# One batch's token turns and the attention scores: the second token block moved behind the scores of step 6, and one maximum moved ahead of the keys' low part

## The chip, the core and the metric

The kernel runs on one core of one Trainium2 chip. The metric is the device time of one execution in microseconds (us); the figure quoted for a kernel is the median of its runs. An execution has five engines that work side by side, each through its own queue in order: TensorE (PE, with its weight loads shown apart as PEld), VectorE (DVE), ScalarE (ACT), GpSimd (POOL) and SyncE (SP), which here only issues DMAs. They wait for one another through semaphores.

## What is computed

Eight batches of 512 tokens of width 512 pass through a cross attention with 16 heads of 32, and then through a layer that mixes eight linear experts by a per-output router. Cut to what matters:

```
x = x + attention(layernorm(x), ctx, Wq, Wkv, Wout)
    qp = q @ Wq.T; k, v = split(ctx @ Wkv.T); per head: softmax(causal(q k^T / sqrt(32))) v; then @ Wout.T
x = x + mix(layernorm(x), router_w, router_b, expert_w, expert_b)
    logits = (h @ router_w.T + router_b).reshape(T, 512, 8); probs = softmax(logits)
    the two largest of eight per output, divided by their sum and added up over the outputs, weigh the eight experts' outputs
```

The causal mask lets query i see keys 0 to i, so only the first 512 context rows are used.

## The kernel before, in words

The attention stage takes about the first 640 us and is where the change lies; the router and expert stage follows, and the change doesn't touch it.

In the attention stage each batch b has four groups c = 0 to 3 of four heads (n = 4b + c counts groups). Each group has eight steps v = 0 to 7. The order on every engine is written by hand: each engine's `body` walks the same grid of (b, c, v) and issues its own share. Batches 1 to 5 are one loop body that the engines repeat (`Fori`), batch 0, 6 and 7 are written out.

All products with fp32 accuracy are made of three: each operand is split in a high part (a rounding, made by ScalarE) and a low part (the rest, made by VectorE). TensorE's three matmuls stand in L268 to L270.

What matters around the change, in c = 0 (`more` is true for batches 0 to 6):

- **First-pass scores** (`scores`, L673, mask matmul L679) run three steps ahead of the softmax. At step v they belong to the step that `target(c, v)` names, so "the scores of step 6" are those that are issued in v = 6. They fill one double bank, `s_ps`. VectorE takes each row's maximum from it (`maxima`, L1395 for masked steps), and the next scores wait for that (`negmax`), as there is just the one double bank.
- **Second-pass scores** (`shifted_scores`, L706) hold the maxima as extra rows; ScalarE takes their exponential (L1100).
- **Keys** of the group three ahead are made in v = 5 in bank 0 of `j_ps`. ScalarE copies their high part (L1017), VectorE makes the low part (`lo_of`, L1383).
- **Turned tokens**: in v = 6 and v = 7 of c = 0 the next batch's four blocks of 128 normalised tokens are transposed on TensorE (`turn_tokens`, `norm_turn`, L626, four matmuls a block). Block i goes to bank 1 - i % 2 of `j_ps`. ScalarE copies the high part (L1008), VectorE makes the low part (`turned_tokens`, L1371), and only then is the bank free. `TURNED` says which blocks in which step: 0 and 1 in v = 6, 2 and 3 in v = 7.
- **Banks**: `take(bank, task, k)` waits for what the bank held last. So block 0 (bank 1) waits for the queries' low part, block 1 (bank 0) for the keys' low part (`k_lo`), block 2 (bank 1) for the low part of block 0, and block 3 (bank 0) for the low part of block 1 (`xT_lo`).
- Behind block 3 in TensorE's queue stand the products with the values (`values_of`, L722), the sums (L734) and the scores of step 7.
- `lo_shift` (L1410) splits the turned maxima; SP's DMAs (L385) copy them into the rows of the second pass.

Of the kernel before, what the change touches and what calls it, by code (L numbers as in the profile page):

```python
# [28 lines left out]
QB = S // P  # L29
# [7 lines left out]
AHEAD = 3  # L37
# [8 lines left out]
def build(nc, x, ctxT, wqT, wkvT, woT, routerT, router_b, expertT, expert_b, out):  # L46
    ctx = ExitStack()
    with ctx:
# [228 lines left out]
        def masked(c, v):  # L277

            return v in (3, 4) or c == 0 and v > 4
# [11 lines left out]
        NORMALISED = ((2, 7), (3, 1), (3, 3), (3, 7))  # L291
        LAST_GROUP = {3: 0, 5: 1, 7: 2}
        TURNED = {6: (0, 1), 7: (2, 3)}
        OUT_BUF = (0, 1, 2, 0)
        INVERTED = 2
        REFINED = 3
# [16 lines left out]
        def key_rest(c):  # L313

            return {0: (0, 5), 1: (1, 7), 2: (2, 7), 3: (3, 7)}[c]
# [298 lines left out]
        def _(pe):  # L614
# [193 lines left out]
            def body(b, first, more, further):  # L808
                last = not more
                held = [("K", b * KC + AHEAD - 1), ("Q", b * KC + AHEAD - 1)]  # L810

                def take(bank, task, k):
                    freed(*held[bank])
                    held[bank] = (task, k)

                for c in range(KC):
                    n = b * KC + c
                    ahead = more or c == 0

                    def project(v):  # L820
                        i, chunk = out_block(c, v, last)
                        if i == 0:

                            pe.wait_ge(s["o_hi"], (b - 1) * KC + chunk + 1)
                            pe.wait_ge(s["o_lo"], (b - 1) * KC + chunk + 1)
                        if chunk == 0:
                            take(0, "WO", (b - 1) * QB + i)
                        project_out(b - 1, i, chunk, 0)

                    def turn_tokens(i):  # L830
                        take(1 - i % 2, "LNT", (b + 1) * QB + i)
                        norm_turn((b + 1) * QB + i, i, 1 - i % 2)

                    for v in range(UNITS):
                        out = not first and out_block(c, v, last) is not None
                        final = last and c == KC - 1
                        shifted_scores(n, c, v, final)
                        g, vv = target(c, v - 1)
                        if not masked((c if v else c - 1) % KC, (v - 1) % UNITS) and (more or c + g < KC):
                            scores(n + g, (c + g) % KC, vv, (1,))  # L840
                        if c == 0 and v in VALUE:
                            take(0, "V", b * QB + VALUE[v])
                            values(VALUE[v])
                        if v in QUERY and ahead:
                            if QUERY[v] == 0:
                                take(1, "Q", n + AHEAD)
                            queries(n + AHEAD, (c + AHEAD) % KC, QUERY[v])
                        if v == SUMMED and not (first and c == 0):
                            finish_group(n - 1, (c - 1) % KC, b if c else b - 1)
                        if final and v in LAST_GROUP:  # L850
                            last_group(LAST_GROUP[v])
                        if v == key_step(c) and ahead:
                            take(key_bank(c), "K", n + AHEAD)
                            keys((c + AHEAD) % KC, b if c == 0 else b + 1, key_bank(c))
                        if c == 0 and more:
                            for i in TURNED.get(v, ()):
                                turn_tokens(i)
                        if v == LAST and not final:
                            values_of(n, c, b, 0)
                            first_sums(n, more or c < KC - 1)  # L860
                            values_of(n, c, b, 1)
                        if out:
                            project(v)
                        g, vv = target(c, v)
                        if more or c + g < KC:
                            if masked(c, v):
                                scores(n + g, (c + g) % KC, vv, mask=True)
                            else:
                                scores(n + g, (c + g) % KC, vv, (0,))
                        if v == TURN and (more or c < KC - 1):  # L870
                            turn_maxima(n + 1, c + 1)

# [461 lines left out]
        def _(dve):  # L1334
# [33 lines left out]
            def turned_tokens(g, i, bank):  # L1368
                dve.wait_ge(s["xT_hi"], g + 1)
                cols = slice(i * P, (i + 1) * P)  # L1370
                dve.tensor_tensor(xnT_l[:, :, cols], j_ps[bank][:].rearrange("p (k q) -> p k q", k=KC),  # L1371
                                  f32(xnT_h[:, :, cols]), ALU.subtract).then_inc(s["xT_lo"], 1)
# [92 lines left out]
            def body(b, first, more, further):  # L1465
                last = not more
                for c in range(KC):
                    n = b * KC + c
                    ahead = more or c == 0
                    for v in range(UNITS):  # L1470
                        if v == TURN + 1 and (more or c < KC - 1):
                            lo_shift(n + 1)
                        if not (first and c == 0):
                            if v == REFINED:
                                refined(n - 1, (c - 1) % KC)
                            if v == SCALED:
                                scaled(n - 1, (c - 1) % KC)
                        i = None if first else summed_block(c, v, last)
                        if i is not None:
                            residual(b - 1, i, 0)  # L1480
                        if (c, v) == key_rest(c) and ahead:
                            lo_of(n + AHEAD, KL, "k", key_bank(c))
                        if c == 0 and more:
                            for i in TURNED.get(v, ()):
                                turned_tokens((b + 1) * QB + i, i, 1 - i % 2)
                        if (c, v) in STATISTICS and further:

                            block_statistics(b + 2, STATISTICS.index((c, v)))
                        g, vv = target(c, v)
                        if more or c + g < KC:  # L1490
                            maxima(n + g, (c + g) % KC, vv, masked(c, v))
                        if QUERY.get(v) == KC - 1 and ahead:
                            lo_of(n + AHEAD, QL, "q", 1)
                        if last:
                            for k, q in FIX_EARLY.get((c, v), ()):
                                fix_router(k, q)
# [470 lines left out]
```

## Time and profile before

| | us |
|---|---|
| median of 3 runs | 1967.65 |
| lowest, highest | 1967.07, 1969.15 |
| the profiled execution, whole time | 1970.22 |
| its span in the trace | 1968.5 |
| mean granted clock of TensorE | 0.993 of full speed |

The profile is of one execution. TensorE is busy nearly all of the span, and most of the chain that ended last is its own work, so the question for any place is whether TensorE gets on with its queue there. A timeline row gives the start in us from the span's start, the duration in us, the engine, the line and the operation; "x4" merges neighbours of one kind, and the bracket at the end is idle time of that engine ahead of the row with what released it. Neighbouring rows overlap a little, because an instruction starts while the one before drains.

### The profile page before, as it was taken

To read this page: it belongs to the slowest core of one execution; us is meant where nothing else is said; L and a number is where in the kernel's file an instruction comes from. 1 tells how busy PE (TensorE), PEld (TensorE's weight loads), DVE (VectorE), ACT (ScalarE), POOL (GpSimd) and SP (SyncE) were. 2 spreads that over 40 slices of the span, in tenths; PEclk is the share of its full clock that TensorE was granted. 3 is DMA by queue.
4 is the path that set the end of the run, shared out by engine and by line. 5 is a ranking of instruction groups with operands and counts; after the bars stand their busy time and mean duration, and the time that the engine had idled before them with its cause. 6 is when DMAs were issued, how large, how long until landed. Compare 5 with 4: busy or idle time off the path is not lost.

```text
span 1968.5 us, 30378 instructions
## 1 busy us (share of the span) xinstructions
PE 1906.8 (97%) x9772; PEld 1512.4 (77%) x9772; DVE 1430.0 (73%) x2840; ACT 1040.6 (53%) x2064; POOL 841.6 (43%) x1016
## 2 busy tenths in 40 slices
PE   4899999999989999999999999999999999999999
PEld 3667777777766788888888888788888888888887
DVE  5677767777667757878788888477777777777752
ACT  2566666566555438777778777543333344333330
POOL 4587777777674133554544354011111232111110
PEclk8999999999999999999999999999999999999999
DMA  5454554455468387867764554822222232222210
GB/s 167 113 125 130 148 145 122 131 150 133 112 161 288 131 252 231 275 226 257 250 219 172 207 196 178 318 89 80 96 85 80 81 109 109 80 85 96 80 43 32
DMA packets 103694, 294.56 MB, mean 150 GB/s; under 512 B 13777, under 2 KB 14801, under 8 KB 98482
## 3 DMA queue, kind: packets, MB, share of 16 engines
q1 hardware_dynamic: 91394, 209.44, 33.1%
q10 hardware_dynamic: 8880, 67.37, 10.5%
q0 software_dynamic: 3328, 16.78, 3.5%
q8 instruction: 26, 0.43, 0.1%
q14 instruction: 66, 0.54, 0.1%
HBM read 150.31 MB, written 109.16 MB: 132 GB/s over the span
## 4 chain that ended last, share of the span: by engine, by line
PE 86%; DVE 6%; DMA 3%; ACT 2%; issue 2%; SPq 1%; POOL 0%; ACTq 0%; DVEq 0%; POOLq 0%
PE pair L268 21%; PE pair L270 21%; PE pair L269 21%; PE pair L673 4%; PE pair L706 4%; PE ps L722 3%; PE ps L268 3%; PE ps L269 3%; PE ps L270 3%; DMA w_raw<-w_fix 1%; DMA xb<-x 1%; PE ps L742 1%; DVE pair L1401 1%; DVE nmax L1395 1%; ACT pT L1100 1%
## 5 line engine op out<-in xcount | busy, mean ns | idle before, releaser
L268 PE MATMUL pair<-w_h,hT 128*128 128x512 f32 x1920 | 751.3, 391 | 6.7 <-DVE w_l L1705 4.7
L270 PE MATMUL pair<-w_h,hT 128*128 128x512 f32 x1920 | 748.2, 390 | 0.0
L269 PE MATMUL pair<-w_l,hT 128*128 128x512 f32 x1920 | 747.7, 389 | 0.0
L1916 POOL TENSOR_TENSOR logits<-logits,second 128x512 f32<-128x512 f32 x224 | 298.3, 1368 | 603.7 <-DVE second L1613 603.4
L268 PEld LDWEIGHTS pair<-w_h,hT 128*128 128x128 f32 x1920 | 360.9, 188 | 83.0 <-issue 9.1
L270 PEld LDWEIGHTS pair<-w_h,hT 128*128 128x128 f32 x1920 | 360.7, 188 | 75.5
L269 PEld LDWEIGHTS pair<-w_l,hT 128*128 128x128 f32 x1920 | 361.0, 188 | 74.0
L1716 DVE SCALAR_TENSOR_TENSOR xb<-pair,c_all,xb 128x512 f32<-128x512 f32 x256 | 191.9, 750 | 179.7 <-PE pair L270 174.8
L1100 ACT ACTIVATE pT<-pair,zero 128x1024 f32<-128x1024 f32 (+3 forms) x256 | 202.6, 792 | 199.3 <-PE pair L706 186.6
L1401 DVE CUSTOM_DVE_ANT_0 pair<-pair,future 128x256 f32<-128x256 f32 (+3 forms) x340 | 184.3, 555 | 122.6 <-PE pair L673 116.1
L1203 ACT ACTIVATE w<-tree 128x512 f32<-128x512 f32 x32 | 20.3, 634 | 408.6 <-DVE tree L1615 408.5
L673 PE MATMUL pair<-qk_st 96*128 96x256 f32 (+3 forms) x512 | 159.6, 342 | 22.2 <-DVE nmax L1395 10.7
L1844 POOL TENSOR_SCALAR_AFFINE_SELECT pT<-pT 128x256 f32<-128x256 f32 x248 | 100.6, 406 | 132.5 <-ACT pT L1100 132.3
L1667 DVE SCALAR_TENSOR_TENSOR scrap<-ps,w 128x512 bf16<-128x512 f32 x224 | 153.3, 685 | 0.8 <-ACT w L1206 0.8
L673 PEld LDWEIGHTS pair<-qk_st 96*128 96x128 f32 x512 | 96.8, 192 | 67.2 <-issue 32.6
L1661 DVE SCALAR_TENSOR_TENSOR ps<-logits,ps 128x512 f32<-128x512 f32 x192 | 133.3, 694 | 16.8 <-DVE scrap L1667 0.5
L1175 ACT ACTIVATE over<-over 128x512 f32<-128x512 f32 x224 | 141.7, 633 | 7.0
L1172 ACT ACTIVATE junk<-over 128x512 bf16<-128x512 f32 x224 | 141.5, 632 | 7.1
L706 PE MATMUL pair<-qk_st 98*128 98x256 f32 (+3 forms) x512 | 133.7, 343 | 6.6 <-ACT pT L1100 4.7
L1167 ACT ACTIVATE over<-logits 128x512 f32<-128x512 f32 x224 | 130.2, 625 | 9.2 <-POOL logits L1916 8.2
L1836 POOL TENSOR_TENSOR acc<-acc,pT 128x512 f32<-128x512 f32 (+1 forms) x124 | 125.0, 1008 | 10.4
L1831 POOL TENSOR_TENSOR acc<-pT,pT 128x768 f32<-128x768 f32 x62 | 114.4, 1845 | 5.2
(165 smaller groups left out, 2604.5 us busy)
## 6 DMA issues: line engine op xcount, KB each, us to landing
logits<-lg_all ACTq DMA_DIRECT2D x32, 1792.0 KB, 8.6
qk_st<-qk SPq DMA_DIRECT2D x372, 128.0 KB, 2.5
lg_all<-ev_a SPq DMA_DIRECT2D x30, 768.0 KB, 8.3
lg_all<-ev_b SPq DMA_DIRECT2D x30, 768.0 KB, 3.7
xb<-x SPq DMA_DIRECT2D x64, 256.0 KB, 4.5
hT_all<-hT SPq DMA_DIRECT2D x32, 512.0 KB, 4.4
hT<-hT_all SPq DMA_DIRECT2D x32, 512.0 KB, 4.0
xt<-in_x SPq DMA_DIRECT2D x8, 1024.0 KB, 5.3
```

The lines of the kernel that those rows point to most:

```text
L268: pe.matmul(dst, lh, rh, start=start, stop=False)
L269: pe.matmul(dst, lh, rl, start=False, stop=False)
L270: return pe.matmul(dst, ll, rh, start=False, stop=stop)
L673: mm = pe.matmul(s_ps[:, j, 0:w], qk_st[c][0:STACK, 0, hh, i * P:w], qk_st[c][0:STACK, 1, hh, 0:w], start=True, stop=not mask)
L706: mm = pe.matmul(dst[:, j, 0:w], qk_st[c][0:STACK + SHIFT_ROWS, 1, hh, kb * P:(kb + 1) * P], qk_st[c][0:STACK + SHIFT_ROWS, 0, hh, kb * P: ...
L1100: act.activation(pT[kb][:, pair:pair + 2, :], src[:, :, 0:S - kb * P], ACT.Exp, bias=zero[:])\
L1172: act.activation(junk[:], over[j][:], ACT.Sign, accum_out=sign_sum[:, i, e:e + 1])\
L1175: act.activation(over[j][:], over[j][:], ACT.Tanh, scale=0.5, accum_out=tanh_sum[:, i, e:e + 1]).then_inc(s["first_step"], 1)
L1401: dve.tensor_tensor_reduce(row, row, future[:, S - (i + 1) * P:S], -1.0, -MASKED, ALU.add, ALU.min, accum_out=nmax[:, c % 2, at:at + 1]).t ...
L1667: dve.scalar_tensor_tensor(scrap[:, e % 2, :], taken_ps[e % 2], 1.0, w2[:], ALU.min, ALU.mult, accum_out=c_taken[:, i, e - 1:e]).then_inc( ...
L1716: dve.scalar_tensor_tensor(xb[i][:], l_ps[e % 4], c_all[:, t, e:e + 1], xb[i][:], ALU.mult, ALU.add).then_inc(s["acc"], 1)
L1916: pool.tensor_tensor(logits[t % 2][:, e - 1, :], logits[t % 2][:, e - 1, :], second[:], ALU.subtract)\
```

## The change

Two things are moved, both in c = 0; no operation is added or taken away, and no buffer changes.

1. Token block 1 (`TURNED_LATE = 1`) is turned at the end of step 6: on TensorE its four transposes come behind the scores of step 6 and not ahead of them, and on VectorE its low part comes behind the maximum of step 6. ScalarE's order is left as it was.
2. On VectorE, in step 5, the maximum of the scores of step 5 comes ahead of the low part of the keys.

```diff
+        TURNED_LATE = 1
 ...
@@ TensorE
                         if c == 0 and more:
                             for i in TURNED.get(v, ()):
-                                turn_tokens(i)
+                                if i != TURNED_LATE:
+                                    turn_tokens(i)
 ...
                                 scores(n + g, (c + g) % KC, vv, (0,))
+                        if c == 0 and more and TURNED_LATE in TURNED.get(v, ()):
+                            turn_tokens(TURNED_LATE)
 ...
@@ VectorE
-                        if (c, v) == key_rest(c) and ahead:
+                        if (c, v) == key_rest(c) and c and ahead:
                             lo_of(n + AHEAD, KL, "k", key_bank(c))
                         if c == 0 and more:
                             for i in TURNED.get(v, ()):
-                                turned_tokens((b + 1) * QB + i, i, 1 - i % 2)
+                                if i != TURNED_LATE:
+                                    turned_tokens((b + 1) * QB + i, i, 1 - i % 2)
 ...
                             maxima(n + g, (c + g) % KC, vv, masked(c, v))
+                        if (c, v) == key_rest(c) and not c and ahead:
+                            lo_of(n + AHEAD, KL, "k", key_bank(c))
+                        if c == 0 and more and TURNED_LATE in TURNED.get(v, ()):
+                            turned_tokens((b + 1) * QB + TURNED_LATE, TURNED_LATE, 1 - TURNED_LATE % 2)
```

TensorE's queue from the turned maxima of step 5 (L688) to token block 2 in batch 0, before. `ps<-ident,xt` is a token block's transpose, `pair<-qk_st_76` the first-pass scores, `pair<-qk_st_74` the second-pass scores of the running group:

```order
123 L688 MATMUL ps<-ident,nmax 16x128 [waits negmax]
124 L706 MATMUL pair<-qk_st_74 128x128 [waits exps]
126 L626 MATMUL ps<-ident,xt 128x128 [waits xn_ok,q_lo,q_hi]
128 L626 MATMUL ps<-ident,xt 128x128 [waits xn_ok,k_lo,k_hi]
130 L673 MATMUL pair<-qk_st_76 128x512 [waits negmax,stacked1]
132 L679 MATMUL pair<-mask_r,ident_r 128x128 x2
133 L706 MATMUL pair<-qk_st_74 128x128 [waits exps]
135 L626 MATMUL ps<-ident,xt 128x128 [waits xn_ok,xT_lo,xT_hi]
137 L626 MATMUL ps<-ident,xt 128x128 [waits xn_ok,xT_lo,xT_hi]
```

The same place of TensorE's queue in the changed kernel, where L627 is L626 of before, L674 is L673, L680 is L679 and L707 is L706:

```order
124 L707 MATMUL pair<-qk_st_74 128x128 [waits exps]
126 L627 MATMUL ps<-ident,xt 128x128 [waits xn_ok,q_lo,q_hi]
128 L674 MATMUL pair<-qk_st_76 128x512 [waits negmax,stacked1]
130 L680 MATMUL pair<-mask_r,ident_r 128x128 x2
131 L627 MATMUL ps<-ident,xt 128x128 [waits xn_ok,k_lo,k_hi]
133 L707 MATMUL pair<-qk_st_74 128x128 [waits exps]
135 L627 MATMUL ps<-ident,xt 128x128 [waits xn_ok,xT_lo,xT_hi]
137 L627 MATMUL ps<-ident,xt 128x128 [waits xn_ok,xT_lo,xT_hi]
```

The block that waits for `k_lo` has moved from row 128 to row 131, behind the scores; the last row, block 3, waits for the low part of block 1 as before.

VectorE's queue at the same place, before: the low part of the keys (L1383), the maxima of steps 5, 6 and 7 (L1395), and the low parts of the token blocks (L1371):

```order
94 L1380 SCALAR_TENSOR_TENSOR qk<-ps,qk 128x512 [waits q_hi]
95 L1383 TENSOR_TENSOR qk<-ps,qk 128x512 [waits k_hi]
96 L1395 TENSOR_REDUCE nmax<-pair 128x2 [waits scores,turned]
97 L1410 TENSOR_TENSOR nm_l<-ps,nm_h 16x128 [waits rows_in,nm_hi]
98 L1371 TENSOR_TENSOR xnT_l<-ps,xnT_h 128x4x128 [waits xT_hi] x2
99 L1395 TENSOR_REDUCE nmax<-pair 128x2 [waits scores]
100 L1371 TENSOR_TENSOR xnT_l<-ps,xnT_h 128x4x128 [waits xT_hi] x2
101 L1395 TENSOR_REDUCE nmax<-pair 128x2 [waits scores]
```

And in the changed kernel, where all line numbers of VectorE are four higher:

```order
94 L1384 SCALAR_TENSOR_TENSOR qk<-ps,qk 128x512 [waits q_hi]
95 L1399 TENSOR_REDUCE nmax<-pair 128x2 [waits scores,turned]
96 L1387 TENSOR_TENSOR qk<-ps,qk 128x512 [waits k_hi]
97 L1414 TENSOR_TENSOR nm_l<-ps,nm_h 16x128 [waits rows_in,nm_hi]
98 L1375 TENSOR_TENSOR xnT_l<-ps,xnT_h 128x4x128 [waits xT_hi]
99 L1399 TENSOR_REDUCE nmax<-pair 128x2 [waits scores]
100 L1375 TENSOR_TENSOR xnT_l<-ps,xnT_h 128x4x128 [waits xT_hi] x3
101 L1399 TENSOR_REDUCE nmax<-pair 128x2 [waits scores]
```

Keys and maximum of step 5 have changed places, and block 1's low part stands behind the maximum of step 6, in front of those of blocks 2 and 3.

## Rows read from the trace of the kernel before

**Rows 1.** The page: busy shares by engine, and the chain's shares by engine.

```profile
PE 1906.8 (97%) x9772; PEld 1512.4 (77%) x9772; DVE 1430.0 (73%) x2840; ACT 1040.6 (53%) x2064; POOL 841.6 (43%) x1016
...
PE 86%; DVE 6%; DMA 3%; ACT 2%; issue 2%; SPq 1%; POOL 0%; ACTq 0%; DVEq 0%; POOLq 0%
```

**Rows 2.** Timeline of TensorE's matmuls, batch 1, steps 5 to 7 of c = 0.

```profile
135.53 0.34 PE L679 MATMUL pair<-mask_r,ident_r 128*128 128x128 f32 x2
...
135.99 0.62 PE L626 MATMUL ps<-ident,xt 128*128 128x128 f32 x4
136.82 0.65 PE L626 MATMUL ps<-ident,xt 128*128 128x128 f32 x4 [0.21 <-DVE qk L1383]
137.78 0.74 PE L673 MATMUL pair<-qk_st 96*128 96x512 f32 x2 [0.30 <-DVE nmax L1395]
...
138.52 0.39 PE L706 MATMUL pair<-qk_st 98*128 98x128 f32 x2
138.75 1.24 PE L626 MATMUL ps<-ident,xt 128*128 128x128 f32 x8
139.92 0.64 PE L722 MATMUL ps<-pT,v_sb 128*32 128x512 f32 x4
```

**Rows 3.** Timeline of TensorE's weight loads: token blocks 2 and 3 there.

```profile
138.73 0.42 PEld L626 LDWEIGHTS ps<-ident,xt 128*128 128x128 f32 x4
139.33 0.42 PEld L626 LDWEIGHTS ps<-ident,xt 128*128 128x128 f32 x4 [0.18 <-issue]
```

**Rows 4.** Timeline of VectorE over the same stretch.

```profile
135.90 0.69 DVE L1383 TENSOR_TENSOR qk<-ps,qk 128x512 fp32r<-128x512 f32 x1 [0.53 <-ACT qk L1017]
136.51 1.22 DVE L1395 TENSOR_REDUCE nmax<-pair 128x2 f32<-128x1024 f32 x1
137.64 0.27 DVE L1410 TENSOR_TENSOR nm_l<-ps,nm_h 16x128 fp32r<-16x128 f32 x1
137.83 1.27 DVE L1371 TENSOR_TENSOR xnT_l<-ps,xnT_h 128x512 fp32r<-128x512 f32 x2
139.03 1.20 DVE L1395 TENSOR_REDUCE nmax<-pair 128x2 f32<-128x1024 f32 x1
140.16 1.27 DVE L1371 TENSOR_TENSOR xnT_l<-ps,xnT_h 128x512 fp32r<-128x512 f32 x2
142.68 0.96 DVE L1395 TENSOR_REDUCE nmax<-pair 128x2 f32<-128x768 f32 x1 [1.25 <-PE pair L679]
```

**Rows 5.** Timeline of ScalarE there: last group's outputs, exponential of step 7, blocks 2, 3.

```profile
138.01 0.62 ACT L1032 ACTIVATE oT_h<-o_sb 128x512 fp32r<-128x512 f32 x1
139.03 0.47 ACT L1100 ACTIVATE pT<-pair,zero 128x256 f32<-128x256 f32 x1 [0.40 <-PE pair L706]
139.43 1.19 ACT L1008 ACTIVATE xnT_h<-ps 128x512 fp32r<-128x512 f32 x2
```

**Rows 6.** The line view of the low parts (L1371), attention stage, start-up left out.

```profile
L1371 DVE TENSOR_TENSOR xnT_l<-ps,xnT_h x28: 667/668/670, 72.3 to 499.1; 128x512 fp32r<-128x512 f32 x28
```

**Rows 7.** TensorE, blocks 2 and 3 of batch 0; the next group's first second-pass scores, batch 1.

```profile
73.29 1.06 PE L626 MATMUL ps<-ident,xt 128*128 128x128 f32 x8
...
142.41 0.68 PE L706 MATMUL pair<-qk_st 98*128 98x512 f32 x2
```

**Rows 8.** Windows: engines' busy us and counts, then granted clock, DMA share, GB/s.

```profile
597.50:601.00 3.50, 2.48 (x16) 2.01 (x15) 2.91 (x5) 1.44 (x2) 3.42 (x4) 0.99 0.43 133
136.60:140.00 3.40, 2.89 (x23) 2.21 (x26) 3.40 (x5) 2.78 (x6) 3.30 (x5) 1.00 0.02 5
601.00:604.40 3.40, 3.40 (x12) 2.62 (x12) 0.70 (x2) 1.44 (x3) 3.23 (x5) 0.51 0.00 0
563.40:566.80 3.40, 2.12 (x14) 1.75 (x13) 2.55 (x4) 2.90 (x6) 3.23 (x5) 1.00 0.01 3
139.90:143.30 3.40, 3.40 (x33) 2.02 (x33) 2.15 (x4) 0.74 (x3) 1.17 (x3) 1.00 0.69 155
```

## The prediction

> **What bounds the kernel now.** I read the page first: TensorE is busy 97% of the span and has 86% of the chain that ended last [rows 1]. So a time on another engine counts only where TensorE stands still for it, and any new standstill of TensorE counts in full unless a later one shrinks. Then I read the timeline of TensorE in the one place that is changed, steps 5 to 7 of c = 0 [rows 2], beside those of its weight loads [rows 3] and of VectorE [rows 4]. The reader is to see two things there.
>
> First, two small waits: token block 1 starts at 136.82, 0.21 behind the end of block 0, since the keys' low part ended at 136.59; and the scores of step 6 start at 137.78, 0.30 behind block 1, since the maximum of step 5 ended at 137.73 [rows 2, 4]. These are what the change works on.
>
> Second, a wait that is not flagged: the loads of block 3 start at 139.33, while those of block 2 (138.73 for 0.42) had ended at 139.15 [rows 3]. Block 3 needs bank 0, which holds block 1 until VectorE has its low part. That ended at 139.10 (two of them, 137.83 to 139.10) [rows 4], 0.23 before the load, the same distance as from the keys' low part (136.59) to block 1 (136.82) [rows 2, 4]. So block 3 already starts at the first moment that VectorE's queue lets it, and there is no slack: whatever delays block 1's low part delays TensorE by the same time. In batch 0 blocks 2 and 3 run from 73.29 for 1.06 [rows 7], without a gap between them, but only just.
>
> From the end of the scores of step 5 to the low part of block 3 VectorE has no gap: 135.90, 136.51, 137.64, 137.83, 139.03, 140.16, to 141.43, each row beginning before the one ahead has ended [rows 4]. It is the engine with no slack in this stretch, and what moves in its queue is what counts.
>
> **The change part by part.** All times are those of batch 1; the 28 low parts of token blocks (4 in each of 7 batches) take 667 to 670 ns each [rows 6], so the place occurs 7 times in the same form, and I price it once and take it seven times.
>
> *VectorE, step 5: maximum ahead of the keys' low part.* The mask matmuls of step 5 end at 135.53 + 0.34 = 135.87; VectorE starts behind such an end by 0.11 elsewhere (142.68 with the idle time in front of it ended by L679 [rows 4]), so the maximum starts at 135.98, not at 136.51, and ends at 137.20. TensorE's scores of step 6 start 0.05 after that, as before (137.73 to 137.78), so at 137.25, earlier by 0.53. In start-to-start times, which rows 4 give (a maximum 1.13, keys' low part 0.61, maxima's low part 0.19, a token block's low part 0.60): keys' low part 137.11 to 137.80, `lo_shift` 137.72, low part of block 0 137.91 to 138.58.
>
> *TensorE, step 6.* Block 0 at 135.99 as before, then a wait until 137.25: 0.64 in one piece, in place of 0.21 and 0.30. The scores of step 6 take their place until about 137.99 (0.74 on, as 137.78 to 138.52 [rows 2]). Block 1 then needs the keys' low part, 137.80 + 0.23 = 138.03. It starts there, and the second-pass scores of step 7 follow at 138.60, where they stood at 138.52. So up to here the change gains nothing: TensorE's work is the same, and both of its waits hang on VectorE, which has the same 1.83 of work (maximum and keys) ahead. I take +0.1.
>
> *VectorE, step 6: block 1's low part behind the maximum.* The maximum of step 6 starts at 137.91 + 0.60 = 138.51 (its scores end some 0.9 after 137.25, in time) and block 1's low part at 139.64, to end at 140.31. Before, it ended at 139.10. The difference is 1.21: one maximum of 1.13, and the 0.08 by which the chain starts later. Its other input is in time: block 1 is on TensorE until 138.68, ScalarE's copy of 0.60 ends at about 139.3.
>
> *TensorE, step 7.* Block 2 needs block 0's low part (138.58 + 0.23 = 138.81) and starts at about 138.87. Block 3 needs block 1's: 140.31 + 0.23 = 140.54, against 139.33 [rows 3]. TensorE stands from about 139.4 to 140.54, and behind block 3 in its queue are the products with the values (139.92 before [rows 2]), the sums and the scores of step 7. **+1.21 us** on each.
>
> *Is it given back?* ScalarE copies block 1 at 138.7 instead of 137.51, and has the outputs (0.62) and then the exponential of step 7 behind it: 139.03 becomes about 139.9 [rows 5]. The exponential of the next group waits for TensorE's second-pass scores, 142.41 before [rows 7], 143.6 now, so this has room. VectorE's low parts of blocks 2 and 3 end at about 142.5, ahead of the maximum of step 7, which had to wait 1.25 for its scores [rows 4] and will again. SP's row copies hang on `lo_shift`, 0.08 later than before; the second-pass scores that need them are later by 1.2. GpSimd hides and adds what ScalarE gives it, and has as much room. All that follows waits for TensorE, so nothing takes the 1.21 back: 7 x 1.21 = **8.5 us**.
>
> *The clock.* After start-up the granted clock fell in this stage once: 601.0 to 604.4 at 0.51, behind a stretch (597.5 to 601.0) in which TensorE was busy 2.48 of 3.50 us, between waits [rows 8]. The place that is changed now has 2.89 of 3.40 at a clock of 1.00 [rows 8]. With the change, the 3.4 us from 137.1 to 140.5 hold the scores of step 6 (137.25 to 138.16), block 1 (to 138.68), the second-pass scores and block 2 (to about 139.55): 2.3 of 3.4, below the stretch that fell. Against it stands 563.4 to 566.8, busy 2.12 of 3.40 without a fall [rows 8], so the busy time alone doesn't decide, and these rows don't tell what does; but the work of 597.5 to 601.0 (score products, narrow mask products, a wait of about 1 us) is the nearer kin. The price of a fall: half the speed (1.2 in place of 2.4 GHz) for the 3.4 us that rows 8 show is up to 1.7, where TensorE is busy throughout as at 139.9 to 143.3 (3.40 of 3.40 [rows 8]), and nothing if it doesn't fall. I take 1.3, since waits lie in some of it, and a fall at 5 of the 7 places, since the counter-example shows that such a stretch can also pass without one: **6.5 us**.
>
> The Trainium skill bears on this in "TensorE: Matmul & The Clock Gate", part 1, "What's actually happening": the half clock is the default and activity is what lifts it, so idle time can bring it back. By that rule each new standstill may cost more than its own length; by the timeline alone, it costs just its length. The trace agrees at 601.0 and gives a counter-example at 563.4.
>
> **Sum.** 8.5 + 6.5 = 15.0. From the profiled execution's own 1970.22 that is 1985.2; the median of the runs lies 2.57 lower, and the same sum on it gives 1967.65 + 15.0 = **1982.6**. 0.2% of it, about what a measurement of this kernel can tell from no change, is 3.9 us.
>
> **The rivals.**
> - *The stall without the clock*: 1967.65 + 8.5 = 1976.1. For it: the counter-example in rows 8. By the skill's rule above it is the case in which the new idle time is too short to matter.
> - *The clock at all seven places, in full*: 8.5 + 7 x 1.7 = 20.4, so 1988.1. For it: the places are alike, and dense work follows each.
> - *Half of it given back*: if the exponentials or the row copies behind the place had room for TensorE to catch up, some 0.6 each: +4.2, 1971.9. Against it: TensorE had no gap from 139.9 to 143.3 that could shrink [rows 8].
> - *Faster*: the maximum ahead of the keys frees the scores of step 6 0.53 earlier, and block 3 is on time. Its most is both waits of now, 0.21 + 0.30 [rows 2], so 7 x 0.51 = 3.6: 1964.0. It decides at one point: block 1's low part would have to be done by 139.10 as before, though a maximum of 1.13 has been put ahead of it on an engine without a gap. That needs VectorE's rows to overlap in a way that rows 4 don't show.
>
> **How the numbers follow.** Chances: stall and clock 0.50 (1982.6), stall alone 0.27 (1976.1), all falls in full 0.10 (1988.1), half given back 0.07, faster 0.06. The range: low end is the stall alone with a fifth less at each place (7 x 1.0 = 7.0, so 1974.6, taken as 1974.5), high end the case of all falls, 1988.5. It leaves out the last two cases and a little of the third. Faster by over 0.2% (below 1963.7): 0.04, most of the last case. Within 0.2%: 0.07, the rest of it and the part of the fourth that ends below 1971.6. Slower: 0.89.
>
> **What the profile of the changed kernel would show.** VectorE in c = 0 of batch 1: maximum, keys' low part, `lo_shift`, one token block, maximum, three token blocks, without a gap until block 2. TensorE: one wait of about 0.6 before the scores of step 6, and a new one of about 1.1 in front of block 3, put down to VectorE's low part (L1375) or to nothing; the products with the values about 1.2 later than block 2's start would have had them. The exponential of step 7 later by 0.9. The granted clock at 0.50 for stretches of some 3.4 us behind some of the seven places. I am wrong if block 3 follows block 2 without a wait, if batches 0 to 6 don't grow by 1.2 or more, or, for the second term, if the clock stays at 1.00 from batch 0 to batch 6.

## The result, and where the time went

The changed kernel is slower: 1982.80 us in the median of 4 runs (1980.67 to 1984.68), against 1968.40 (4 runs, 1967.07 to 1971.07), a ratio of 1.0070 with a 95% interval of 1.0057 to 1.0082. That is +14.4; 15.0 was forecast. A later comparison gave less: 1980.47 (6 runs) against 1969.91 (23 runs), 1.0048 (1.0034 to 1.0063), +10.6. Over all 11 runs of the changed kernel and the 79 of before that have a clock on record, on several chips, the medians are 1980.87 and 1968.93, +11.9.

The page hardly moves. It has TensorE at 96% with 1908.3 us busy, so the time is not new work but new standing. TensorE's timeline in batch 1, to be laid beside [rows 2]:

```profile
137.09 0.62 PE L627 MATMUL ps<-ident,xt 128*128 128x128 f32 x4
138.39 0.72 PE L674 MATMUL pair<-qk_st 96*128 96x512 f32 x2 [0.67 <-DVE nmax L1399]
138.95 0.34 PE L680 MATMUL pair<-mask_r,ident_r 128*128 128x128 f32 x2
139.17 0.65 PE L627 MATMUL ps<-ident,xt 128*128 128x128 f32 x4
139.57 0.42 PE L707 MATMUL pair<-qk_st 98*128 98x128 f32 x2
139.95 0.65 PE L627 MATMUL ps<-ident,xt 128*128 128x128 f32 x4
141.68 0.65 PE L627 MATMUL ps<-ident,xt 128*128 128x128 f32 x4 [1.08 <-DVE xnT_l L1375]
142.26 1.07 PE L723 MATMUL ps<-pT,v_sb 128*32 128x512 f32 x8
```

The two small waits have become one of 0.67 in front of the scores, and a wait of 1.08 now stands in front of block 3, put down to VectorE's low part of a token block. From the start of block 0 to the products with the values it is 142.26 - 137.09 = 5.17; it was 139.92 - 135.99 = 3.93. So 1.24 a place. VectorE's timeline of the same stretch [rows 4]:

```profile
137.11 1.23 DVE L1399 TENSOR_REDUCE nmax<-pair 128x2 f32<-128x1024 f32 x1 [0.64 <-PE ps L689]
138.25 0.68 DVE L1387 TENSOR_TENSOR qk<-ps,qk 128x512 fp32r<-128x512 f32 x1
138.85 0.27 DVE L1414 TENSOR_TENSOR nm_l<-ps,nm_h 16x128 fp32r<-16x128 f32 x1
139.05 0.67 DVE L1375 TENSOR_TENSOR xnT_l<-ps,xnT_h 128x512 fp32r<-128x512 f32 x1
139.64 1.20 DVE L1399 TENSOR_REDUCE nmax<-pair 128x2 f32<-128x1024 f32 x1
140.78 0.67 DVE L1375 TENSOR_TENSOR xnT_l<-ps,xnT_h 128x512 fp32r<-128x512 f32 x1
141.86 0.69 DVE L1375 TENSOR_TENSOR xnT_l<-ps,xnT_h 128x512 fp32r<-128x512 f32 x1 [0.41 <-ACT xnT_h L1012]
```

No gap from 137.11 to block 1's low part, which ends at 141.45; block 3 starts 0.23 later. To see what else there is, the span of each trace is cut in three: from the first turned maxima to those that are issued in step 5 of batch 7's first group (it holds all seven places), from there to the first router product (the last batch and the turn-over), and the rest. The column "falls there" names the falls of the granted clock to half in the second stretch, each 3.4 us long unless another length is given. Worked out from the starts of the matmuls in the traces:

| trace | places | last batch | falls there | rest |
|---|---|---|---|---|
| before | 514.23 | 68.56 | 601.0 | 1334.86 |
| before, second trace | 513.68 | 66.94 | none | 1336.30 |
| changed | 523.08 | 69.77 | 577.0, 611.1 | 1335.17 |
| changed, second trace | 522.53 | 70.58 | 580.1 (6.8 us) | 1335.05 |
| changed, third trace | 522.42 | 72.11 | 582.8 (6.8 us) | 1335.35 |

The places cost 522.68 - 513.96 = **8.7 us** in the mean, 1.25 each. The last batch costs another 3.1 in these traces. The rest is level.

The last batch has no token blocks, but the change acts in it too: its second part hangs on c = 0 alone and not on `more`, so in step 5 of batch 7's first group VectorE's maximum comes ahead of the keys' low part as well. What that does stands under "More traces of the two kernels".

In none of the 21 places of the three changed traces did the clock fall. The window over the two new waits, in batch 1 and in batch 2 (columns as in [rows 8]), beside one of the falls of the last batch:

```profile
137.10:141.70 4.60, 2.85 (x21) 2.19 (x20) 4.33 (x6) 3.04 (x7) 3.17 (x5) 1.00 0.03 7
138.20:141.60 3.40, 2.21 (x14) 1.78 (x14) 3.25 (x6) 1.94 (x5) 2.06 (x4) 1.00 0.02 5
...
210.60:215.20 4.60, 2.85 (x21) 2.19 (x20) 4.33 (x6) 3.05 (x7) 3.19 (x5) 1.00 0.02 4
...
577.00:580.40 3.40, 3.40 (x25) 1.19 (x18) 0.88 (x1) 0.28 (x1) 2.30 (x3) 0.50 0.99 353
```

TensorE is busy 2.85 of 4.60 us there, and the clock stays at 1.00. The second row is the stretch for which the prediction had written 2.3 busy of 3.4, with this trace's times: it has 2.21.

### The profile page after: what moved, and what is told of

Its sections match the earlier page's. It is cut to its first block, busy times and chain, and to the rows that moved or that the text cites. A ratio compares the mean times of both kernels' runs of the same rounds, so it can differ in the third digit from the quotient of the medians.

```text
span 1978.9 us, 30378 instructions
## 1 busy us (share of the span) xinstructions
PE 1908.3 (96%) x9772; PEld 1513.3 (76%) x9772; DVE 1431.5 (72%) x2840; ACT 1040.2 (53%) x2064; POOL 842.6 (43%) x1016
## 3 DMA queue, kind: packets, MB, share of 16 engines
q10 hardware_dynamic: 8880, 67.37, 10.5%
## 4 chain that ended last, share of the span: by engine, by line
PE 85%; DVE 6%; DMA 3%; issue 2%; ACT 2%; SPq 1%; POOL 0%; ACTq 0%; DVEq 0%; POOLq 0%
PE pair L268 21%; PE pair L270 21%; PE pair L269 21%; PE pair L674 4%; PE pair L707 3%; PE ps L723 3%; PE ps L268 3%; PE ps L269 3%; PE ps L270 3%; DMA w_raw<-w_fix 1%; DMA xb<-x 1%; PE ps L743 1%; DVE pair L1405 1%; DVE nmax L1399 1%; ACT pT L1104 1%
## 5 line engine op out<-in xcount | busy, mean ns | idle before, releaser
L674 PE MATMUL pair<-qk_st 96*128 96x256 f32 (+3 forms) x512 | 159.7, 342 | 24.1 <-DVE nmax L1399 12.5
L674 PEld LDWEIGHTS pair<-qk_st 96*128 96x128 f32 x512 | 96.9, 193 | 69.9 <-issue 34.1
L707 PE MATMUL pair<-qk_st 98*128 98x256 f32 (+3 forms) x512 | 133.9, 343 | 6.7 <-ACT pT L1104 5.0
L1845 POOL TENSOR_TENSOR acc<-acc,pT 128x512 f32<-128x512 f32 (+1 forms) x124 | 125.1, 1009 | 10.3
```

The costliest lines, as they stand in the source:

```text
L674: mm = pe.matmul(s_ps[:, j, 0:w], qk_st[c][0:STACK, 0, hh, i * P:w], qk_st[c][0:STACK, 1, hh, 0:w], start=True, stop=not mask)
L707: mm = pe.matmul(dst[:, j, 0:w], qk_st[c][0:STACK + SHIFT_ROWS, 1, hh, kb * P:(kb + 1) * P], qk_st[c][0:STACK + SHIFT_ROWS, 0, hh, kb * P: ...
```

## Experiments

The theory is that of the prediction: TensorE's block 3 waits for VectorE's low part of block 1, and any delay of that counts in full. Its second half is that the clock falls behind the new standstill. Each kernel is set against runs of before that were made along with its own.

### The maximum first, alone

```diff
-                        if (c, v) == key_rest(c) and ahead:
+                        if (c, v) == key_rest(c) and c and ahead:
                             lo_of(n + AHEAD, KL, "k", key_bank(c))
 ...
                             maxima(n + g, (c + g) % KC, vv, masked(c, v))
+                        if (c, v) == key_rest(c) and not c and ahead:
+                            lo_of(n + AHEAD, KL, "k", key_bank(c))
```

> Only the second part of the change: VectorE's maximum of step 5 ahead of the keys' low part; token block 1 stays ahead of the scores of step 6. Queue theory (block 3 waits for block 1's low part): block 1 now waits for the keys' low part until about 138.0 in the times of before (136.8 before), its low part ends at about 140.0 in place of 139.1, block 3 starts 0.9 later, so 7 x 0.9 = +6.3 us, and a little more where the clock falls behind it. Rival (the maximum moved ahead is a gain, the loss comes from block 1's move alone): within 1 us of before or faster by up to 3.6.

Measured: 1978.34 against 1968.92, 1.0046 (1.0031 to 1.0061), +9.4. The places take 520.36, 6.4 more than before's 513.96: the +6.3 of the queue theory. The remainder is the last batch (71.07, with a wait of 2.96 for a row copy and falls at 578.9 and 630.1).

```profile
135.77 0.62 PE L626 MATMUL ps<-ident,xt 128*128 128x128 f32 x4
137.84 0.65 PE L626 MATMUL ps<-ident,xt 128*128 128x128 f32 x4 [1.45 <-DVE qk L1383]
138.25 0.71 PE L673 MATMUL pair<-qk_st 96*128 96x512 f32 x2
```

In TensorE's timeline block 1, still ahead of the scores, waits 1.45 for the keys' low part, which the maximum has pushed back. So this half is no gain by itself; with block 1 ahead it can't let the scores go earlier at all.

### Block 1 late, alone

```diff
 (the changed kernel, with this of before put back on VectorE)
-                        if (c, v) == key_rest(c) and c and ahead:
+                        if (c, v) == key_rest(c) and ahead:
                             lo_of(n + AHEAD, KL, "k", key_bank(c))
 ...
-                        if (c, v) == key_rest(c) and not c and ahead:
-                            lo_of(n + AHEAD, KL, "k", key_bank(c))
```

> Only the first part of the change: token block 1 behind the scores and the maximum of step 6, on TensorE and VectorE; the keys' low part stays ahead of the maximum of step 5. Queue theory: scores of step 6 start when they did (137.78), the maximum of step 6 only at about 138.8, block 1's low part ends at about 140.6, block 3 starts 1.5 later: 7 x 1.5 = +10.5 us, plus what the clock adds. Rival (the two parts have prices of their own that add up to the whole): the difference of the whole and of the maximum alone, so about +8.

Measured: 1979.95 against 1968.92, 1.0056 (1.0041 to 1.0072), +11.0; places 524.75, +10.8; last batch 66.89, without a fall. The queue theory's +10.5 holds, and the rival's sum of parts (+8) does not: 10.8 and 6.4 don't add up to the 8.7 of the two together. With the maximum first, block 1's move costs 2.3 on top (8.7 - 6.4) and not 10.8: both act on the same queue. This kernel waits 1.16 before the scores of step 6 and 1.06 before block 3, and its clock doesn't fall at any place.

### Only VectorE's low part of block 1 late

```diff
                             for i in TURNED.get(v, ()):
-                                turned_tokens((b + 1) * QB + i, i, 1 - i % 2)
+                                if i != 1:
+                                    turned_tokens((b + 1) * QB + i, i, 1 - i % 2)
 ...
                             maxima(n + g, (c + g) % KC, vv, masked(c, v))
+                        if c == 0 and more and v == 6:
+                            turned_tokens((b + 1) * QB + 1, 1, 0)
```

> The kernel before, with one thing moved: VectorE makes the low part of token block 1 behind the maximum of step 6; TensorE's order is that of before. Queue theory: block 3 starts one maximum later, 1.13 us, at each of the 7 places: batches longer by 1.1 in the trace, +7.9 us plus or minus what the clock does. Rival (the loss needs block 1's turn to be late on TensorE too): batches as long as before.

Measured: 1984.91 (3 runs) against 1968.73, 1.0081 (1.0064 to 1.0097), +16.2, where +7.9 and something for the clock was expected. Its trace is the only one in which the clock did fall at the changed place, in 4 of 7: at 74.7, 289.8, 364.9 and 440.0.

```profile
288.04 0.65 PE L626 MATMUL ps<-ident,xt 128*128 128x128 f32 x4
290.14 1.11 PE L626 MATMUL ps<-ident,xt 128*128 128x128 f32 x4 [1.46 <-DVE xnT_l L1371]
```

```profile
289.80:293.20 3.40, 3.06 (x20) 1.39 (x24) 1.40 (x3) 0.60 (x1) 0.65 (x1) 0.50 0.84 189
...
440.00:443.40 3.40, 3.40 (x26) 0.99 (x24) 0.69 (x1) 0.60 (x1) 0.00 (x0) 0.50 0.88 202
```

The timeline shows the wait (1.46) and that block 3's four transposes behind it take 1.11 where 0.65 is usual; the windows show the granted clock at 0.50. Batches without a fall are 73.14 and 73.20 us apart, those with one 74.59, 74.79 and 74.69: a fall costs 1.4 to 1.6 us here. The wait itself costs 1.5 a place and not the 1.13 of my expectation, as VectorE stood 0.28 before the maximum of step 6 for its scores:

```profile
213.93 0.67 DVE L1371 TENSOR_TENSOR xnT_l<-ps,xnT_h 128x512 fp32r<-128x512 f32 x1
214.88 1.23 DVE L1395 TENSOR_REDUCE nmax<-pair 128x2 f32<-128x1024 f32 x1 [0.28 <-PE pair L679]
```

With 7 x 1.5 = 10.5 and 4 falls of 1.5 the sum is 16.5; the trace's places take 531.06, +17.1.

### Block 3 behind work that is ready

```diff
 (on top of the changed kernel, TensorE)
-                                if i != TURNED_LATE:
+                                if i not in (TURNED_LATE, 3):
                                     turn_tokens(i)
 ...
                             first_sums(n, more or c < KC - 1)
+                            if c == 0 and more:
+                                turn_tokens(3)
                             values_of(n, c, b, 1)
```

> The changed kernel, with token block 3 issued on TensorE behind the products with the values of key block 0 and the first sums (about 1.1 us of work), in place of ahead of them. Nothing else moves. Queue theory: block 1's low part is then ready when TensorE comes to block 3, no wait of over 0.2 is left in front of it, and the 1.2 us a batch go: 1967 to 1970 us, level with before or up to 1 us faster. Rival (the time is lost elsewhere, by ScalarE's later exponential of step 7 or by the clock whatever stands there): over 1975 us.

Measured: 1974.35 (11 runs) against 1968.92, 1.0024 (1.0015 to 1.0033), +5.4. The stall is gone:

```profile
138.50 0.65 PE L627 MATMUL ps<-ident,xt 128*128 128x128 f32 x4
139.08 1.07 PE L723 MATMUL ps<-pT,v_sb 128*32 128x512 f32 x8
139.97 0.40 PE L735 MATMUL ps<-pT,ones 128*32 128x128 f32 x8
140.30 0.66 PE L627 MATMUL ps<-ident,xt 128*128 128x128 f32 x4
140.88 0.85 PE L723 MATMUL ps<-pT,v_sb 128*32 128x384 f32 x8
```

Block 3 follows the sums without an idle time flagged, and the places take 515.77, 6.9 less than the changed kernel's 522.68. So the wait in front of block 3 is the cause of four fifths of the 8.7. But the kernel isn't level with before, as I had written: 1.8 remain at the places (about 1.1 of it because the wait of 0.67 before the scores is 0.16 longer than the two that it took the place of), and the last batch takes 72.04, with a wait of 3.69 for a row copy and falls at 576.1 and 627.3. Neither theory had the whole right.

### The stall filled with useless work

```diff
 (on top of the changed kernel; TensorE is kept busy ahead of block 3)
+                                if i == 3:
+                                    fill(n)
 ...
+                    def fill(n):
+                        pe.wait_ge(s["nm_hi"], n + 2)
+                        pe.wait_ge(s["nm_lo"], n + 2)
+                        for k in range(FILLS):          # FILLS = 4
+                            pe.matmul(d_ps[:], wq_h[:, k, 0:P], wq_h[:, k, :], start=True, stop=True)
```

> The changed kernel, with four 128x512 matmuls of no use (about 0.23 us each) issued on TensorE in front of block 3, into a bank that is free there; they end before block 1's low part is ready, so the wait is shorter but block 3 starts when it did. Clock theory (the part of the loss above 8.5 us comes from a clock that falls behind the standstill in some runs): mean granted clock up to 0.993 or more in all runs, time 1976 to 1979 us, with less spread than the changed kernel's 4.0 us. Rival (the rest isn't the clock): 1981 to 1985 us, with clocks as in the changed kernel.

Measured: 1984.47 (5 runs, 1980.83 to 1985.44) against 1968.92, 1.0078 (1.0064 to 1.0092), with clocks of 0.989 to 0.992.

```profile
139.14 0.65 PE L628 MATMUL ps<-ident,xt 128*128 128x128 f32 x4
139.55 1.18 PE L840 MATMUL ps<-wq_h 128*128 128x512 f32 x4
140.87 0.65 PE L628 MATMUL ps<-ident,xt 128*128 128x128 f32 x4
```

The fill works as meant, block 3 starts 4.58 to 4.62 behind block 0 in batches 1 to 5 and 4.45 in 0 and 6, nearly as in the changed kernel. The places take 521.65, 1.0 less, all of it from the start-up: one of its falls of the clock is 3.4 us long here (at 55.2) and 6.8 in the others. The time isn't lower and the clock isn't better; the trace is of the fastest of the five runs, and what the slower ones did can't be seen. So what the changed kernel loses beyond 8.7 isn't a clock that falls behind the standstill. This is where the second half of my theory fell.

### Does a delay cost its length?

```diff
 (on top of before: batch 6 alone, ahead of block 3; `fill` as above, FILLS = 7 or 15)
+                                if i == 3 and not further:
+                                    fill(n)
                                 turn_tokens(i)
```

> The kernel before, with seven 128x512 matmuls of no use in one place, in front of token block 3 of batch 6; TensorE is busy with them, so no wait is added anywhere and batches 0 to 5 are untouched. 7 x 0.23 = 1.6 us of work. Alignment theory (what the clock costs in batch 7 and behind it depends on when these stages begin): the time moves by something else than 1.6, by up to 3 us more, with a mean granted clock below the 0.9928 of before. Rival (a delay counts by its length, and the further 3.8 us of the kernel with block 3 behind the sums come from its changed places): +1.6 us, clock as before.

> As the kernel with seven extra matmuls in front of block 3 of batch 6, with fifteen: 3.4 us of work. Alignment theory: the excess over 3.4 is another than the excess of the seven, and may be nothing. Rival (a delay counts by its length): +3.4 us, twice that of the seven and a little more.

Measured: 1971.34 (10 runs), 1.0015 (1.0005 to 1.0025), +2.6 for 1.6 us of work; and 1974.15 (9 runs), 1.0034 (1.0024 to 1.0044), +5.4 for 3.4 us. The places take 516.09 and 517.41, that is +2.1 and +3.5, about the length of the work. The excess of the medians is 1.0 and 2.0, with mean clocks of 0.9914 and 0.9911 over their runs, against 0.9925 over those of before. Before run against itself differed by 1.1 (below), so the excess of the seven is no more than noise, and that of the fifteen little more. Inconclusive in the times. In the traces the last batch takes 69.10 and 68.50, with falls of the clock but without a late row copy, so starting it 1.6 or 3.4 us later did not bring the remainder of the changed kernel.

### More traces of the two kernels

> The changed kernel once more, for a second trace of it. If the clock falls behind the new standstills, falls stand in batches 0 to 6 here though not in the first trace; if it falls only later, all falls after start-up lie beyond batch 6, and block 3 starts 4.58 us behind block 0 in each batch again.

> The changed kernel once more, timed in more rounds, for the clocks of many executions. If the time above the two traces (about 1980.5) is the clock, the slower executions have the lower mean granted clocks: a fall of 3.4 us at half speed is 0.0009 of the mean clock and, by the batches of the kernel with only block 1's low part late, about 1.5 us. So 1980 to 1981 at 0.992 to 0.993 and some 3 us more at 0.990. Rival: no tie between time and clock.

> The kernel before once more, for a second trace of it. If what the clock costs behind batch 6 varies from execution to execution in any kernel, this trace has its falls in batch 7 elsewhere than at 601.0, and from the turned maxima of batch 7's first group on it takes another time than the 68.6 us of the first trace (31.2 + 17.8 + 19.5), while batches 1 to 6 are 71.6 us apart as there. Rival (the falls come with the kernel, not with the execution): a fall at 601 again and 68.6 us again.

The second changed trace: 1980.41, all falls beyond batch 6, block 3 at 4.58 or 4.59 in batches 1 to 5 (4.45 in 0 and 6). The third comparison is the one quoted at the top; by the granted clock its six executions are 1981.70, 1981.93 (0.991), 1978.78, 1980.08, 1978.31 (0.992) and 1980.87 (0.990). Within these six the tie is weak: 1980.87 has the lowest clock, where some 3 us more was expected. Over all runs, time against clock:

| clock | before, mean us (runs) | changed, mean us (runs) |
|---|---|---|
| 0.994 | 1967.99 (11) | |
| 0.993 | 1968.58 (30) | |
| 0.992 | 1969.56 (27) | 1980.15 (6) |
| 0.991 | 1971.33 (7) | 1982.20 (3) |
| 0.990 | 1972.96 (4) | 1982.78 (2) |

In either kernel time goes with the clock, and at the same clock the change costs 10.6, 10.9 and 9.8. That is more than the 8.7 of the places.

Before, second time: 1969.60 (10 runs) against 1968.51, 1.0005 (0.9995 to 1.0014). Its trace has no fall in the last batch, which takes 66.94 in place of 68.56, with batches 71.6 apart as in the first. The trace with block 1 late alone has 66.89, and that with the low part late 66.93, without a fall as well. All eleven others lie above, at 67.93 to 72.11, and all have one. But the clock isn't all of it. A fall of 6.8 us to half speed takes at most 3.4 us of TensorE's work, and the third changed trace, which has such a fall, lies 5.2 above the floor of 66.9.

The other part is a wait for a row copy, the transfer of the maxima's low part (L385, 8 KB) into the rows of the second pass of batch 7's second group. Before, second trace:

```profile
566.32 0.59 SPq L385 DMA_DIRECT2D qk_st<-nm_l  x1
566.72 0.39 ACTq L992 DMA_DIRECT2D w_raw<-in_routerT  x1
570.08 0.73 PE L706 MATMUL pair<-qk_st 98*128 98x512 f32 x2 [0.83 <-DMA qk_st<-nm_l]
```

The changed kernel, third trace:

```profile
575.31 0.39 ACTq L996 DMA_DIRECT2D w_raw<-in_routerT  x1
575.50 0.59 SPq L386 DMA_DIRECT2D qk_st<-nm_l  x1
581.55 0.73 PE L707 MATMUL pair<-qk_st 98*128 98x512 f32 x2 [3.71 <-DMA qk_st<-nm_l]
```

In batch 7 no token block stands in the way, so the maximum first does let the scores of step 6 go earlier, by 0.5, and with them ScalarE's exponential of step 7. Right behind that in its queue ScalarE has the transfer of 1 MB of router weights, which it issues at 575.31 where the exponential starts at 575.30. `lo_shift` and the row copy are 0.1 later. So the two transfers have changed places, and the row copy lands 6.0 us behind its issue in place of 3.7. That splits all 14 traces by kernel, and not by execution:

| VectorE in step 5 | traces | router weights issued | row copy takes | last batch |
|---|---|---|---|---|
| maximum first (changed, maximum alone, block 3 behind the sums, stall filled) | 6 | 0.2 ahead of the row copy | 5.1 to 6.0 | 69.8 to 72.1 |
| keys first (all others) | 8 | 0.4 to 0.8 behind it | 3.6 to 4.1 | 66.9 to 69.1 |

The second-pass scores that need the copy start 8.6 us behind the turned maxima in the mean of the three changed traces and 6.9 in the two of before: 1.7 to 1.8 of the 3.1. All six traces of the upper row also have a fall of the clock that begins within 10.3 us of those turned maxima, and two of the eight others do. With the 8.7 of the places this makes 10.4 to 10.5, near the 9.8 to 10.9 that the change costs at the same clock. That the router weights' transfer is what holds the copy up is read from the order in the traces; no run moved it alone.

### Filling the waits with work that is due anyway

```diff
 (on top of before, TensorE, c = 0)
                             for i in TURNED.get(v, ()):
+                                if i == 1:
+                                    values_of(n, c, b, 0)
                                 turn_tokens(i)
 ...
                         if v == LAST and not final:
-                            values_of(n, c, b, 0)
+                            if not (c == 0 and more):
+                                values_of(n, c, b, 0)
```

> The kernel before, with the products of the values with key block 0 (0.88 us of TensorE) in c = 0 issued in step 6, between token blocks 0 and 1, in place of step 7. They need nothing that is late there. Queue theory: they cover the two waits of 0.2 and 0.3 and what stands beside them, VectorE's chain is as before, and TensorE gets to the scores of step 7 up to 1.0 us earlier at 7 places: 1962 to 1966 us. Rival (TensorE's work is only moved, and block 3's wait for VectorE grows by as much): 1968 us.

Measured: 1966.88 (12 runs) against 1969.91, 0.9986 (0.9975 to 0.9996), -3.0: faster than both kernels, but short of the 1962 to 1966 of the expectation.

```profile
135.09 1.06 PE L722 MATMUL ps<-pT,v_sb 128*32 128x512 f32 x8
136.09 0.66 PE L626 MATMUL ps<-ident,xt 128*128 128x128 f32 x4
136.50 0.71 PE L673 MATMUL pair<-qk_st 96*128 96x512 f32 x2
137.05 0.34 PE L679 MATMUL pair<-mask_r,ident_r 128*128 128x128 f32 x2
137.22 0.38 PE L706 MATMUL pair<-qk_st 98*128 98x128 f32 x2
137.44 0.63 PE L626 MATMUL ps<-ident,xt 128*128 128x128 f32 x4
138.33 0.65 PE L626 MATMUL ps<-ident,xt 128*128 128x128 f32 x4 [0.26 <-DVE xnT_l L1374]
```

Neither block 1 nor the scores wait, and batches are 71.25 apart where they were 71.64. The gain a place is 0.4 and not 1.0, since block 1's turn on TensorE is later, VectorE stands 0.36 for it, and a wait of 0.26 is left at block 3: the same queue again.

The same in the other groups, the products behind the second-pass scores of step 5:

```diff
                         shifted_scores(n, c, v, final)
+                        if v == TURN and c and more:
+                            values_of(n, c, b, 0)
 ...
                         if v == LAST and not final:
-                            if not (c == 0 and more):
+                            if not more:
                                 values_of(n, c, b, 0)
```

> The same in all groups of batches 0 to 6: in c = 1 to 3 the products with key block 0 go right behind the second-pass scores of step 5, where TensorE waits about 0.4 us for a maximum. If those waits are covered too, up to 0.4 at 21 further places: 1955 to 1960 us. Rival (in those groups the scores of step 5 are on VectorE's path, and delaying them delays the chain by what is gained): level with the kernel that does it in c = 0 alone, or slower.

Measured: 1974.46 (12 runs) against 1969.91, 1.0020 (1.0010 to 1.0029). The rival holds: batches are 72.15 apart, 0.9 longer than with c = 0 alone. The two waits of 0.39 for a maximum are gone from each batch, but VectorE wants the scores of step 5 for the maxima of the row copies, and TensorE now waits for such a copy at the start of each batch:

```profile
194.93 0.73 PE L706 MATMUL pair<-qk_st 98*128 98x512 f32 x2 [0.84 <-DMA qk_st<-nm_l]
```

This wait is 0.78 to 0.95 in batches 1 to 7; with c = 0 alone none is flagged there.

## Why the prediction was right, and where not

- **The unflagged wait was the point on which all hung.** Block 3 started 0.23 behind block 1's low part before the change and does so after it (batches 1 to 5; in 0 and 6, which are written out, 0.16 before and 0.10 after, so there it had 0.06 to spare). The prediction had block 3 4.55 behind block 0 (140.54 - 135.99); the trace has 141.68 - 137.09 = 4.59. The scores were to start 1.26 behind block 0, and did at 1.30; block 1 was to follow them by 0.78, and did.
- **The first term** (7 x 1.21 = 8.5) measured 8.7. That nothing is given back held: the rest is level. ScalarE's exponential of step 7 moved from 3.04 to 3.78 behind block 0, 0.7 where 0.9 was written, without effect. VectorE did get gaps, of 0.41 and 0.45 for ScalarE, at the low parts of blocks 2 and 3; the maximum of step 7 had room for them.
- **The second term was wrong in its place.** "A fall at 5 of the 7 places" was none in 21. The total came out within 0.6 of the first comparison, and that was luck: the part beyond 8.7, which is 5.7 in the first comparison and 3.2 over all runs, isn't made of that. The step that failed is the one that took the stretch of 597.5 to 601.0 for the nearer kin and set the counter-example aside: with the columns of [rows 8] the new stretch has 2.85 of 4.60 busy and no fall. The price of a fall, 1.3, was about right where one was seen (1.4 to 1.6), and falls behind such a wait do exist, in the kernel whose wait is 1.46 and not 1.08.
- **What the remainder is**: the prediction priced seven places and left batch 7 at nothing, though the second part of the change acts there. In the traces the last batch costs 3.1: 1.7 to 1.8 of it is the row copy that lands late behind the router weights, the rest is falls of the clock, some of them behind that wait. The prediction had looked at the row copies, but only where the token blocks follow, and found room. It fits that the kernels with the maximum first lie 3.0 to 7.9 above the cost of their places in the medians, and the others 0.9 below to 1.9 above. A kernel with the change left out of batch 7 alone was not run. Executions without a trace may also have falls at the places; that can't be seen.
- **The rivals**: *stall alone* (1976.1) is what the places cost, and lies below every median. *Half given back* would have been 4.2 at the places, which cost 8.7; *all seven falls* is excluded by the clock at 1.00. *Faster* is excluded by each part taken alone.

## What to carry to other kernels

Before moving a step in a queue, look for waits that the profile doesn't flag: a start that comes at the same distance behind another engine's end in every batch (0.23 here) is a wait with no slack, and every instruction put ahead of that end costs its full length. The queue that has no gap is the one in which order matters; here VectorE's, and a maximum put ahead of one low part cost 7 x 1.2 us. To fill a wait on the bound engine, take work that is long ready and that nobody waits for (the products with key block 0 in c = 0), and not, as in the other groups, a place whose successor another engine is waiting for. And price a moved step at each place where its condition holds: in batch 7, where its neighbours are missing, it changed which of two transfers was issued first.

## What the hardware showed that was not expected

- A fall of the granted clock to half for 3.4 us cost 1.4 to 1.6 us behind the wait of 1.46. In the last batch, in traces whose row copy was on time, one fall cost 1.0 (at 603.3) and 1.6 (624.5), against the 66.9 without one.
- A row copy of 8 KB landed 3.6 to 4.1 us behind its issue when it was issued ahead of a transfer of 1 MB (8 traces), and 5.1 to 6.0 when it was issued 0.2 behind it (6 traces).
- The same kernel on the same chip varies by 3 to 7 us from run to run (before: 3.2, 3.7, 5.0 and 7.2 us between lowest and highest in four comparisons), and that goes with a mean granted clock between 0.990 and 0.994. A difference of 2 us needs more than three runs a side.
- The length of a wait didn't decide whether the clock fell. 1.08 us of standstill beside one of 0.67 left it at 1.00 in 21 of 21 places. With VectorE's low part late alone, where the waits in front of block 3 were 1.34 to 1.49, it fell in or just behind them in 4 of 7, and two of the three without a fall were 1.45 as well. With the maximum first alone, waits of 1.31 to 1.45 in front of block 1 had no fall in 7 of 7. TensorE's busy time doesn't part them either: 2.85 of 4.60 us without a fall, 4.68 of 6.30 (283.5 to 289.8) ahead of one.
